# Attention: the products with picked probabilities are issued half a step later, right ahead of the next weighted products

## The chip, the cores and the metric

The kernel runs on one core of one Trainium2 chip. The metric is the device time of one execution in microseconds (us). The engines have short names in what follows: PE is TensorE, DVE is VectorE, ACT is ScalarE, POOL is GpSimd and SP is SyncE, which issues most of the transfers.

## The reference

Two graph layers are applied, one after the other, to 16 samples of 512 nodes with 128 features each. The first one (two rounds of masked softmax over a graph, a norm, a feed-forward part and a norm) is not touched by the change. The second one is attention with eight heads in which the entry of an integer matrix, `adj`, says which of four value projections an edge uses:

```python
scores = jnp.einsum('bhid,bhjd->bhij', q, k) / np.sqrt(dh)
attn = jax.nn.softmax(scores, axis=-1)
for r in range(Wv.shape[0]):
    v_r = (src @ Wv[r] + bv[r]).reshape(Bb, Nn, h, dh).transpose(0, 2, 1, 3)
    mask = (adj_matrix == r)[:, None]
    out = out + jnp.einsum('bhij,bhjd->bhid', attn * mask, v_r)
attn_out = out.transpose(0, 2, 1, 3).reshape(Bb, Nn, Dm) @ Wo + bo
x = _ln(src + attn_out, g1, beta1)
```

A last feed-forward part and a norm follow. In the data here `adj` holds 0 and 1 alone.

## The kernel before, in words

The kernel has three stages: `graph_layer`, `attention` and `feed_forward`. The change lies in `attention`, which takes about 640 us of the span.

`attention` has two paths and picks one at run time. Path 0 serves inputs with the codes 0 and 1 alone, and it is the one that runs here. It computes `prob` times `val` (the **weighted products**, value projection 0) plus `picked` times `dval` (the **products with picked probabilities**, with `picked = prob * mask` and the difference of projections 1 and 0).

A sample is worked on in a *turn* of eight *steps* (S = 8). Step s stands for head group g = s // 4 (four heads) and key chunk c = s % 4 (128 keys). For every step there are:

- four *peaks* (`peaks`, L990 to L1001 on PE): a bf16 product into `peak[hh % 2]`, of which DVE takes the maximum (L1248). They run six steps ahead of the scores, and there are two `peak` banks. So PE's peak number n waits until DVE has read peak n - 2.
- two *scores* (`scores`, L1015): two bf16 products each. ACT takes their exponential into `prob[s % 2]` (`exps`, L1113).
- `pick`: `picked[s % 2] = prob * mask`. POOL does three heads (L1384) in its step s, DVE the fourth (L1262) in its step s + 1.
- `weigh` (L1019 to L1042 on PE): eight f32 instructions on tiles 32 columns wide, all into `o_ps`, once with `prob` and `val` (`rel` is None) and once with `picked` and `dval` (`rel` is 0). The four chunks of a group accumulate in `o_ps`, and then ACT copies it out (`keep_o`, L1116 to L1124).
- *items*: the other work of the sample, one or two to a step, after a table. On PE every one of them writes the one bank `misc`, so each first waits on `misc_read`: until ACT or DVE has read the item before it. The place of an item in a step is "early", "mid" or "late":

```python
0: [(0, "mid", "q", 2), (1, "mid", "k", 2), (2, "early", "top1", 0), (2, "late", "v0", 1), (3, "mid", "o1", -1),
    (4, "early", "turn_o", -1), (4, "mid", "out", -1), (5, "mid", "y", -1), (6, "early", "top0", 1),
    (6, "late", "v1", 1), (7, "mid", "o0", 0)],
```

The order of each engine is written out by hand in a function `turn`. With P0 to P3 for the peaks, S0 and S1 for the scores, W for the weighted products and Wp for the picked ones, PE's step s (L1082 to L1098) is

P0, S0, [early item], P1, W of step s - 1, P2, S1, [mid item], P3, Wp of step s - 1, [late item].

DVE's step s is: read P0, read P1, pick of step s - 1, early item, read P2, read P3, mid item (L1343 to L1362). In step 5 it adds `norm_stats` (L1323, L1328). ACT's step s is: `exps` of S0, the late item of the step before, early item, in some steps part of a cast or of a mask, `exps` of S1, mid item, `keep_o`, and in steps 0 and 7 `centre` (L1196).

The readers of the items are: q and k, ACT L1134 and then DVE L1300; top0 and top1, DVE L1291 and L1293; v0 and v1, ACT L1142 and L1143; o0 and o1, DVE L1306 and L1310; turn_o, ACT L1155; out, DVE L1314; y, ACT L1157, after the second `exps` of its step.

The semaphore `picked_used` counts the Wp blocks that PE has done. Before the change it guards `picked` (for DVE and POOL) and also `prob`: `exps` of step s waits for Wp of step s - 2.

Of the kernel before, what the change touches and what calls it, by code (L numbers as in the profile page):

```python
# [821 lines left out]
def attention(nc, block, z, w, xs, codes, other, scratch, first_qk, sem, keep):  # L822
# [13 lines left out]
    with ExitStack() as ctx:  # L836
# [3 lines left out]
        def ps(name, shape, dt=F32):  # L840
            return ctx.enter_context(nc.psum_tensor("b_" + name, shape, dt))

        B, N, D, C, H, DH, R = z.B, z.N, z.D, z.C, HEADS, z.DH, z.R
# [44 lines left out]
            0: [(0, "mid", "q", 2), (1, "mid", "k", 2), (2, "early", "top1", 0), (2, "late", "v0", 1), (3, "mid", "o1", -1),  # L888
                (4, "early", "turn_o", -1), (4, "mid", "out", -1), (5, "mid", "y", -1), (6, "early", "top0", 1),
                (6, "late", "v1", 1), (7, "mid", "o0", 0)],  # L890
            1: [(0, "mid", "q", 2), (0, "late", "v0", 0), (0, "late", "v1", 0), (0, "late", "v2", 0), (0, "late", "v3", 0),
                (1, "mid", "k", 2), (2, "early", "top1", 0), (3, "mid", "o1", -1), (4, "early", "turn_o", -1),
                (4, "mid", "out", -1), (5, "mid", "y", -1), (6, "early", "top0", 1), (7, "mid", "o0", 0)],
        }
# [35 lines left out]
        def moved(b, par, s, by):  # L930

            return b + (s + by) // S, (par + (s + by) // S) % 2, (s + by) % S
# [50 lines left out]
        def _(pe):  # L983
# [3 lines left out]
            def run(path, rels):  # L987
                NR = len(rels)

                def peaks(b, par, s, hh):  # L990

                    b, par, s = moved(b, par, s, LEAD)
                    if not live(b):
                        return
                    g, c = s // C, s % C
                    h = GH * g + hh
                    if s == 0 and hh == 0:
                        pe.wait_ge(sem("stacked"), 32 * (b + 1))
                    past(pe, sem("peak_read"), (S * b + s) * GH + hh - 1)
                    pe.matmul(peak[hh % 2][:, :], q_stack[par][0:K, h, c * P:(c + 1) * P], k_stack[par][0:K, h, :],  # L1000
                              start=True, stop=True).then_inc(sem("peak_ready"), 1)  # L1001

                def scores(b, par, s, u):

                    if not live(b):
                        return
                    g, c = s // C, s % C
                    if isinstance(b, int) and b == 0 and s == 0 and u == 0:
                        pe.wait_ge(consts, 4 + R)
                    if c == 0 and u == 0:  # L1010
                        pe.wait_ge(sem(f"tops_in{g}"), 32 * (b + 1))
                    past(pe, sem("exp_ready"), 2 * (S * b + s) + u - 1)
                    for k in range(2):
                        h = GH * g + 2 * u + k
                        mm = pe.matmul(score[u][:, k, :], k_stack[par][:, h, c * P:(c + 1) * P], q_stack[par][:, h, :],  # L1015
                                       start=True, stop=True)
                    mm.then_inc(sem(f"score_ready{u}"), 1)

                def weigh(t, par, s, rel):  # L1019

                    b, par, s = moved(t, par, s, -1)
                    if not live(b):
                        return
                    g, c = s // C, s % C
                    if rel is None:
                        pe.wait_ge(sem("exp_ready"), 2 * (S * b + s) + 2)
                        if s == 0:

                            pe.wait_ge(sem("misc_read"), reads_before(path, *((b - 1, "v1") if path == 0 else (b, "v3"))) + 1)
                        if c == 0:  # L1030
                            past(pe, sem("o_t_ready"), G * b + g)
                        src, v = prob[s % 2], val[par]
                    else:
                        n = NR * (S * b + s) + rel
                        pe.wait_ge(sem("picked_pool"), POOL_HEADS * (n + 1))
                        pe.wait_ge(sem("picked_dve"), (GH - POOL_HEADS) * (n + 1))
                        src, v = picked[(NR * s + rel) % 2], dval[par if path == 0 else rel]
                    for hh in range(GH):
                        mm = pe.matmul(o_ps[32 * hh:32 * hh + 32, :], v[:, c, GH * g + hh, :], src[:, hh, :],  # L1039
                                       start=(c == 0 and rel is None), stop=(c == C - 1 and rel == NR - 1))  # L1040
                    if rel is not None:
                        mm.then_inc(sem("picked_used"), 1)  # L1042

                def item(t, name, by):
                    b = t + by
                    if not live(b):
                        return

                    past(pe, sem("misc_read"), reads_before(path, t, name))
                    if name in ("q", "k"):  # L1050
                        mm = pe.matmul(misc[:, :], w["w" + name][:, :], xs[:, b, :, :].rearrange("p c d -> p (c d)"),
                                       start=True, stop=True)
                    elif name[0] == "v":

                        pe.wait_ge(sem("x_own"), 16 * (b + 1))
                        per, rs = (2, 2) if path == 0 else (1, R)
                        for k in range(per):
                            c = per * int(name[1]) + k
                            at = misc[:, k * rs * D:(k + 1) * rs * D]
                            pe.matmul(at, w["ones"][:, :], w["bias3"][:, 0:rs * D], start=True, stop=False)  # L1060
                            mm = pe.matmul(at, x_own[:, c * P:(c + 1) * P], w["wv"][:, 0:rs, :].rearrange("p r d -> p (r d)"),
                                           start=False, stop=True)
                    elif name[:3] == "top":
                        g = int(name[3])
                        pe.wait_ge(sem("peak_read"), (S * b + (g + 1) * C) * GH)
                        mm = pe.transpose(misc[0:GH * C, 0:P], top[g][:, :, :].rearrange("p h c -> p (h c)"), ident[:, :])
                    elif name in ("o0", "o1"):
                        g = int(name[1])
                        pe.wait_ge(sem("o_t_ready"), G * b + g + 1)
                        for c in range(C):  # L1070
                            mm = pe.transpose(misc[:, c * P:(c + 1) * P], o_t[g][:, c * P:(c + 1) * P], ident[:, :])
                    elif name == "turn_o":
                        for c in range(C):
                            mm = pe.transpose(misc[:, c * P:(c + 1) * P], o[:, c, :], ident[:, :])
                    elif name == "out":
                        mm = pe.matmul(misc[:, :], w["wo"][:, :], o_all_t[:, :], start=True, stop=True)
                    elif name == "y":
                        for c in range(C):
                            mm = pe.transpose(misc[:, c * P:(c + 1) * P], y_t[:, c * P:(c + 1) * P], ident[:, :])
                    mm.then_inc(sem(name + "_done"), 1)  # L1080

                def turn(b, par):  # L1082
                    for s in range(S):
                        peaks(b, par, s, 0)
                        scores(b, par, s, 0)
                        for name, by in items(path, s, "early"):
                            item(b, name, by)
                        peaks(b, par, s, 1)
                        weigh(b, par, s, None)
                        peaks(b, par, s, 2)  # L1090
                        scores(b, par, s, 1)
                        for name, by in items(path, s, "mid"):
                            item(b, name, by)
                        peaks(b, par, s, 3)
                        for rel in range(NR):
                            weigh(b, par, s, rel)
                        for name, by in items(path, s, "late"):
                            item(b, name, by)  # L1098
                turns(pe, turn)
            both_paths(pe, run)  # L1100

        @block.scalar
        def _(act):
            def run(path, rels):
                NR = len(rels)

                def exps(b, s, u):
                    if not live(b):
                        return
                    if u == 0:  # L1110
                        past(act, sem("picked_used"), NR * (S * b + s - 1))
                    act.wait_ge(sem(f"score_ready{u}"), S * b + s + 1)
                    act.activation(prob[s % 2][:, 2 * u:2 * u + 2, :], score[u][:, :, :], ACT.Exp,  # L1113
                                   scale=float(DH) ** -0.5).then_inc(sem("exp_ready"), 1)

                def keep_o(b, par, s):  # L1116

                    b, par, s = moved(b, par, s, -1)
                    if not live(b) or s % C != C - 1:
                        return  # L1120
                    g = s // C
# [76 lines left out]

                def turn(b, par):
                    for s in range(S):  # L1200
                        exps(b, s, 0)
                        if path == 0 and s > 0:
                            for name, by in items(path, s - 1, "late"):
# [11 lines left out]
                            load_tops(b, par, name, by)  # L1215
                        for name, by in items(path, s, "mid"):
                            item(b, par, name, by)
                        keep_o(b, par, s)
                        if path == 1:
                            for name, by in items(path, s, "late"):  # L1220
                                item(b, par, name, by)
# [419 lines left out]
```

## Time and profile before

| | us |
|---|---|
| median of 3 runs | 1255.81 (1253.42 to 1255.83) |
| the profiled execution | 1248.62, of which 1246.8 span |
| busy over the span | PE 87%, DVE 77%, ACT 61%, POOL 49% |
| granted TensorE clock, mean over the span | 0.96 |

The page is read so: "busy" is the union of an engine's instructions. For PE the ends are modelled and instructions overlap, so the distance from one start to the next is the better price. In rows of the timeline the first number is the start in us, the second the length of the merged run, and the number in square brackets is the idle time ahead of it, with what ended it.

### The profile page before, as it was taken

How to read it: one execution, taken by the hardware profiler on the slowest of the kernel's cores; microseconds unless marked ns; L12 is line 12 of the kernel's file. 1: busy time of each engine (PE TensorE's matmuls, PEld its weight loads, DVE VectorE, ACT ScalarE, POOL GpSimd, SP SyncE). 2: the span in 40 equal slices, each digit the busy share in tenths (PEclk: the TensorE clock that was granted, in tenths of full speed). 3: DMA queues.
4: the chain of work that ended last, by engine and by line, in shares of the span. 5: the costliest groups of instructions: out<-in, count | busy, mean ns of one | idle time of the engine just before them, and what ended most of it. 6: DMA issues, size and time to landing. Idle time of an engine off the chain costs nothing. (4 is left out here: it accounts for less than half of the span.)

```text
span 1246.8 us, 21668 instructions
## 1 busy us (share of the span) xinstructions
PE 1087.4 (87%) x6087; PEld 500.5 (40%) x6087; DVE 956.3 (77%) x2313; ACT 758.9 (61%) x1405; POOL 610.5 (49%) x499
## 2 busy tenths in 40 slices
PE   4588877888787649999999999999999999979996
PEld 3565665665564312233333333323333233234442
DVE  2878778778877548788888888888888888618777
ACT  3477677777777324666666666666666666644442
POOL 3313212212300135878887788877888787900000
PEclk8699999999999858999999999999999999979998
DMA  5221112112100242321333213332133320000000
GB/s 171 89 86 68 50 66 86 50 50 101 50 1 1 85 117 72 106 76 43 109 110 105 66 49 110 110 98 68 54 110 110 90 71 9 2 0 34 34 34 34
DMA packets 49413, 86.50 MB, mean 69 GB/s; under 512 B 8787, under 2 KB 35795, under 8 KB 44246
## 3 DMA queue, kind: packets, MB, share of 16 engines
q1 hardware_dynamic: 46454, 85.56, 22.2%
q10 hardware_dynamic: 2912, 0.40, 0.2%
q8 instruction: 20, 0.33, 0.1%
q14 instruction: 27, 0.22, 0.1%
HBM read 52.12 MB, written 29.36 MB: 65 GB/s over the span
## 5 line engine op out<-in xcount | busy, mean ns | idle before, releaser
L1384 POOL TENSOR_TENSOR b_picked<-b_prob,b_mask 128x512 f32<-128x512 f32 x384 | 473.4, 1260 | 128.2 <-ACT b_prob L1113 128.1
L1248 DVE TENSOR_REDUCE b_top<-b_peak 128x1 f32<-128x512 f32 x512 | 343.1, 687 | 86.2 <-PE b_peak L1000 81.5
L1113 ACT ACTIVATE b_prob<-b_score 128x1024 f32<-128x1024 f32 x256 | 262.0, 1023 | 192.7 <-PE b_score L1015 190.8
L381 POOL TENSOR_SCALAR a_code<-a_adj_in 128x512 bf16<-128x512 int32 x64 | 89.0, 1391 | 249.2 <-DMA a_adj_in<-in_adj 245.4
L1039 PE MATMUL b_o_ps<-b_picked,b_dval 128*32 128x512 f32 x1024 | 136.4, 604 | 12.8 <-DVE b_picked L1262 10.2
L1039 PE MATMUL b_o_ps<-b_prob,b_val 128*32 128x512 f32 x1024 | 136.3, 604 | 0.3 <-ACT b_o_t L1124 0.3
L1262 DVE TENSOR_TENSOR b_picked<-b_prob,b_mask 128x512 f32<-128x512 f32 x128 | 113.5, 886 | 1.5 <-ACT b_prob L1113 1.4
L1000 PE MATMUL b_peak<-shared 96*128 96x512 bf16 x256 | 101.3, 399 | 4.7 <-DVE b_top L1248 4.5
L678 DVE CUSTOM_DVE_ANT_0 a_att<-a_att,a_no_edge 128x512 f32<-128x512 f32 x128 | 102.2, 816 | 0.0
L1000 PE MATMUL b_peak<-b_k_stack,b_q_stack 96*128 96x512 bf16 x256 | 98.3, 384 | 0.0
L650 ACT ACTIVATE a_att<-a_att,a_least 128x512 f32<-128x512 f32 x128 | 90.6, 711 | 0.0
L493 PE MATMUL a_turn<-a_hw_n,a_att 128*128 128x128 f32 x512 | 62.3, 281 | 25.7 <-ACT a_hw_n L599 25.6
L1501 ACT ACTIVATE c_hid<-c_mid,bff 128x512 f32<-128x512 f32 x64 | 44.0, 687 | 61.9 <-PE c_mid L1479 61.9
L1015 PE MATMUL b_score<-b_q_stack,b_k_stack 98*128 98x512 bf16 x256 | 76.5, 379 | 0.0
L1015 PE MATMUL b_score<-shared 98*128 98x512 bf16 x256 | 76.4, 379 | 0.0
L493 PEld LDWEIGHTS a_turn<-a_hw_n,a_att 128*128 128x128 f32 x512 | 59.7, 195 | 38.0 <-issue 38.0
L485 PE MATMUL a_out<-a_hid,wff 128*128 128x512 f32 x128 | 59.2, 605 | 18.0 <-ACT a_hid L644 18.0
L479 PE MATMUL a_mid<-a_h_t,wff 128*128 128x512 f32 x128 | 63.0, 617 | 11.1 <-ACT a_h_t L569 11.1
L1000 PEld LDWEIGHTS b_peak<-shared 96*128 96x128 bf16 x256 | 25.0, 98 | 113.0 <-DVE b_top L1248 98.6
L1000 PEld LDWEIGHTS b_peak<-b_k_stack,b_q_stack 96*128 96x128 bf16 x256 | 24.6, 96 | 108.8 <-DVE b_top L1248 93.8
L503 PE MATMUL a_pair<-a_xw_n,a_att 128*128 128x130 f32 x512 | 62.0, 280 | 3.4 <-DVE a_xw_n L710 3.4
L503 PEld LDWEIGHTS a_pair<-a_xw_n,a_att 128*128 128x128 f32 x512 | 60.5, 196 | 3.8 <-issue 3.8
(176 smaller groups left out, 1703.2 us busy)
## 6 DMA issues: line engine op xcount, KB each, us to landing
a_adj_in<-in_adj SPq DMA_DIRECT2D x16, 1024.0 KB, 5.2
scratch<-shared SPq DMA_DIRECT2D x32, 384.0 KB, 2.7
shared<-scratch SPq DMA_DIRECT2D x16, 768.0 KB, 6.7
scratch<-shared SPq DMA_DIRECT2D x32, 256.0 KB, 2.8
b_q_stack<-scratch SPq DMA_DIRECT2D x8, 768.0 KB, 5.4
b_k_stack<-scratch SPq DMA_DIRECT2D x8, 768.0 KB, 8.1
a_x_in<-in_x SPq DMA_DIRECT2D x16, 256.0 KB, 2.7
xs<-in_x SPq DMA_DIRECT2D x16, 256.0 KB, 5.3
```

Of the source, the lines that this page charges most:

```text
L381: eng.tensor_scalar(code[:, c, :].rearrange("p (k q) -> p k q", k=C), adj_in[:, c, :].rearrange("p (q k) -> p k q", k=C), CODE_HI, CODE_LO ...
L493: mm = pe.matmul(turn[:, ic * D:(ic + 1) * D], att[1][:, jc, ic * P:(ic + 1) * P], hw_n[:, jc, :], start=(jc == 0), stop=(jc == C - 1))
L503: mm = pe.matmul(pair[:, ic // 2, at:at + D + 2], att[0][:, jc, ic * P:(ic + 1) * P], xw_n[:, jc, :], start=(jc == 0), stop=(jc == C - 1))
L650: act.activation(att[k][:, c, :], att[k][:, c, :], ACT.Exp, bias=least[k][:, c:c + 1], scale=-1.0, accum_out=total[k][:, c:c + 1]).then_in ...
L678: dve.tensor_tensor_reduce(att[k][:, c, :], att[k][:, c, :], no_edge[:, c, :], 1.0, HIGHEST, ALU.add, ALU.min, least[k][:, c:c + 1]).then_ ...
L1000: pe.matmul(peak[hh % 2][:, :], q_stack[par][0:K, h, c * P:(c + 1) * P], k_stack[par][0:K, h, :], start=True, stop=True).then_inc(sem("pea ...
L1015: mm = pe.matmul(score[u][:, k, :], k_stack[par][:, h, c * P:(c + 1) * P], q_stack[par][:, h, :], start=True, stop=True)
L1039: mm = pe.matmul(o_ps[32 * hh:32 * hh + 32, :], v[:, c, GH * g + hh, :], src[:, hh, :], start=(c == 0 and rel is None), stop=(c == C - 1 a ...
L1113: act.activation(prob[s % 2][:, 2 * u:2 * u + 2, :], score[u][:, :, :], ACT.Exp, scale=float(DH) ** -0.5).then_inc(sem("exp_ready"), 1)
L1248: dve.tensor_reduce(top[g][:, hh, c:c + 1], peak[hh % 2][:, :], AX.X, ALU.max, negate=True).then_inc(sem("peak_read"), 1)
L1262: dve.tensor_tensor(picked[(NR * s + rel) % 2][:, hh, :], prob[s % 2][:, hh, :], m, ALU.mult).then_inc(sem("picked_dve"), 1)
L1384: pool.tensor_tensor(picked[(NR * s + rel) % 2][:, hh, :], prob[s % 2][:, hh, :], m, ALU.mult).then_inc(sem("picked_pool"), 1)
```

## The change

Wp in PE's step s is now that of step s - 2. It is issued right ahead of W, behind P1, except in steps 1 and 5 (`s % C == 1`), in which it is issued at the very start, ahead of P0. The order of PE is then:

- steps 1 and 5: Wp of s - 2, P0, S0, [early], P1, W of s - 1, P2, S1, [mid], P3, [late];
- the six others: P0, S0, [early], P1, Wp of s - 2, W of s - 1, P2, S1, [mid], P3, [late].

W now increments a semaphore of its own, `weighed`. `exps` waits for `weighed` and for POOL's and DVE's picks of step s - 2 in place of `picked_used`. `keep_o` moves from the end of ACT's step to the start of the next one. The rest of the diff puts the value items of path 1, which doesn't run here, into the next step.

```diff
-            1: [(0, "mid", "q", 2), (0, "late", "v0", 0), (0, "late", "v1", 0), (0, "late", "v2", 0), (0, "late", "v3", 0),
+            1: [(0, "mid", "q", 2), (1, "early", "v0", 0), (1, "early", "v1", 0), (1, "early", "v2", 0), (1, "early", "v3", 0),
...
                 def weigh(t, par, s, rel):
 
-                    b, par, s = moved(t, par, s, -1)
+                    b, par, s = moved(t, par, s, -1 if rel is None else -2)
...
-                    if rel is not None:
-                        mm.then_inc(sem("picked_used"), 1)
+                    mm.then_inc(sem("weighed" if rel is None else "picked_used"), 1)
...
                 def turn(b, par):
                     for s in range(S):
+                        ends = s % C == 1
+                        if ends:
+                            weigh_picked(b, par, s)
                         peaks(b, par, s, 0)
                         scores(b, par, s, 0)
                         for name, by in items(path, s, "early"):
                             item(b, name, by)
                         peaks(b, par, s, 1)
+                        if not ends:
+                            weigh_picked(b, par, s)
                         weigh(b, par, s, None)
                         peaks(b, par, s, 2)
                         scores(b, par, s, 1)
                         for name, by in items(path, s, "mid"):
                             item(b, name, by)
                         peaks(b, par, s, 3)
-                        for rel in range(NR):
-                            weigh(b, par, s, rel)
                         for name, by in items(path, s, "late"):
                             item(b, name, by)
+
+                def weigh_picked(b, par, s):
+
+                    for rel in range(NR):
+                        weigh(b, par, s, rel)
...
                     if u == 0:
-                        past(act, sem("picked_used"), NR * (S * b + s - 1))
+                        past(act, sem("picked_pool"), POOL_HEADS * NR * (S * b + s - 1))
+                        past(act, sem("picked_dve"), (GH - POOL_HEADS) * NR * (S * b + s - 1))
+                        past(act, sem("weighed"), S * b + s - 1)
...
                 def keep_o(b, par, s):
 
-                    b, par, s = moved(b, par, s, -1)
+                    b, par, s = moved(b, par, s, -2)
...
                 def turn(b, par):
                     for s in range(S):
+                        keep_o(b, par, s)
                         exps(b, s, 0)
...
                         for name, by in items(path, s, "mid"):
                             item(b, par, name, by)
-                        keep_o(b, par, s)
```

## Rows read from the trace of the kernel before

**Rows 1.** Steady attention: busy us (instructions) of PE, PEld, DVE, ACT, POOL; clock; DMA

```profile
485.30:1053.40 568.10, 558.33 (x3318) 174.04 (x3316) 481.50 (x866) 369.19 (x572) 463.40 (x380) 1.00 0.29 84
```

**Rows 2.** Waits in attention: us in total, times, longest

```profile
PE b_o_ps L1039 <- DVE b_picked L1262: 10.2, 15, 0.8
```

**Rows 3.** Timeline of PE, steps 5 and 6 of one turn

```profile
697.70 0.60 PE L1079 MATMUL b_misc<-ident,shared 128*128 128x128 f32 x4
698.13 0.38 PE L1000 MATMUL b_peak<-shared 96*128 96x512 bf16 x1
698.45 1.06 PE L1039 MATMUL b_o_ps<-b_picked,b_dval 128*32 128x512 f32 x8
699.44 0.39 PE L1000 MATMUL b_peak<-shared 96*128 96x512 bf16 x1
699.67 0.60 PE L1015 MATMUL b_score<-b_q_stack,b_k_stack 98*128 98x512 bf16 x2
700.11 0.27 PE L1066 MATMUL b_misc<-ident,b_top 128*16 128x128 f32 x1
700.22 0.38 PE L1000 MATMUL b_peak<-shared 96*128 96x512 bf16 x1
...
703.25 1.06 PE L1039 MATMUL b_o_ps<-b_picked,b_dval 128*32 128x512 f32 x8 [0.69 <-DVE b_picked L1262]
```

**Rows 4.** Timeline of PE, the two halves of one W block

```profile
706.31 0.64 PE L1039 MATMUL b_o_ps<-b_prob,b_val 128*32 128x512 f32 x4
...
706.76 0.61 PE L1039 MATMUL b_o_ps<-b_prob,b_val 128*32 128x512 f32 x4
```

**Rows 5.** Timeline, item k of step 1 and who reads it

```profile
717.17 1.02 PE L1051 MATMUL b_misc<-xs,wk 128*128 x2
...
718.03 0.38 PE L1000 MATMUL b_peak<-shared 96*128 96x512 bf16 x1
718.29 0.68 ACT L1134 ACTIVATE shared<-b_misc,bk 128x512 bf16<-128x512 f32 x1
...
718.45 0.69 DVE L1248 TENSOR_REDUCE b_top<-b_peak 128x1 f32<-128x512 f32 x1 [0.82 <-PE b_peak L1000]
719.06 0.75 DVE L1300 SCALAR_TENSOR_TENSOR shared<-b_misc,bk,shared 128x512 f32<-128x512 f32 x1
```

**Rows 6.** Timeline, P3 of step 3 and DVE's read of item o1

```profile
727.65 0.38 PE L1000 MATMUL b_peak<-b_k_stack,b_q_stack 96*128 96x512 bf16 x1
...
728.96 0.42 DVE L1310 TENSOR_TENSOR shared<-b_misc,b_inv 128x256 f32<-128x256 f32 x1
```

**Rows 7.** Timeline, ACT, DVE and POOL behind item y of step 5

```profile
698.82 0.58 ACT L1157 COPY b_y<-b_misc 128x512 f32<-128x512 f32 x1
...
701.40 3.83 POOL L1384 TENSOR_TENSOR b_picked<-b_prob,b_mask 128x512 f32<-128x512 f32 x3 [0.71 <-ACT b_prob L1113]
...
701.95 1.16 DVE L1262 TENSOR_TENSOR b_picked<-b_prob,b_mask 128x512 f32<-128x512 f32 x1
...
703.34 0.28 DVE L1293 TENSOR_TENSOR b_top_lo<-b_misc,b_top_hi 16x128 bf16<-16x128 f32 x1
```

**Rows 8.** All picks of DVE: duration ns min/median/max, first and last start

```profile
L1262 DVE TENSOR_TENSOR b_picked<-b_prob,b_mask x128: 681/683/1548, 484.3 to 1090.5; 128x512 f32<-128x512 f32 x128
```

**Rows 9.** Timeline ahead of the first step, when peaks wait for DVE's reads

```profile
466.26 0.68 DVE L1248 TENSOR_REDUCE b_top<-b_peak 128x1 f32<-128x512 f32 x1
...
467.00 0.61 PE L1000 MATMUL b_peak<-shared 96*128 96x512 bf16 x1 [0.21 <-DVE b_top L1248]
```

**Rows 10.** Timeline around the copy of o_ps in steps 0 and 1

```profile
713.52 0.69 ACT L1134 ACTIVATE shared<-b_misc,bq 128x512 bf16<-128x512 f32 x1
...
714.68 0.59 ACT L1124 COPY b_o_t<-b_o_ps 128x512 f32<-128x512 f32 x1 [0.47 <-PE b_o_ps L1039]
715.16 0.88 ACT L1196 ACTIVATE xs<-b_y,b_shift,b_rstd 128x128 f32 x2
...
715.51 1.07 PE L1039 MATMUL b_o_ps<-b_prob,b_val 128*32 128x512 f32 x8
```

## The prediction

> **What bounds the kernel now.** I read the busy time by stretches first. In the steady part of attention PE is busy 558.33 of 568.10 us at the full granted clock, DVE 481.50, POOL 463.40, ACT 369.19 [rows 1]. So PE sets the pace there, and all its idle time is 9.8 us. The view of waits says where that is: Wp waits for DVE's pick, 15 times, 10.2 us [rows 2]. The timeline shows it at one place of each turn, step 6 [rows 3]. The other waits fall on weight loads, which lie beside running products. PE therefore gets faster only if its stream gets shorter, and slower by every wait that is put into it. Prices on PE are start to start.
>
> **What the change takes away.** (a) The wait of Wp in step 6: Wp of step 4 stands there now, whose pick was made a step earlier. That is 10.2 us [rows 2], if nothing behind it waits for the same chain.
>
> (b) Changes between tile shapes. A peak before S0 costs 0.23 (699.44 to 699.67), and before Wp 0.32 (698.13 to 698.45) [rows 3]: 0.09 more to go to 32-column tiles. A block of eight costs 0.99 up to the peak (698.45 to 699.44) [rows 3], but its two halves are 0.45 apart [rows 4], so 2 x 0.45 = 0.90 would do: 0.09 more to leave. With Wp and W adjacent, one entry and one exit vanish: 0.18 per merged step. There are 127 Wp blocks with a W of the next step behind them; those in steps 1 and 5 aren't merged, which leaves 96: 96 x 0.18 = 17.3 us. No row shows two blocks in a row, so the price is bounded: 0 if the second block pays the same again, 17.3 if it costs its halves alone. I take 17.3, since all eight instructions have the shape of those before them, as the two halves do.
>
> The Trainium skill (TensorEngine Tiling (Array Packing), Key Properties) says that changing the tiling mode, and not just the tile, drains TensorE. The two 0.09 us agree. By that rule, which speaks of the switch and not of waits, the change is a gain; it is the first rival.
>
> **What the change puts in.** A Wp block stood between P3 of a step and P0 of the next, and gave DVE and ACT 1.0 us to read what the mid item and P3 had left. It is gone from there in six of eight transitions. From P3 to an early item is now P3, P0, S0, so 0.22 + 0.22 + 0.44 = 0.88 (S0's two instructions of 512 columns take 0.44, 699.67 to 700.11, a peak is one such [rows 3]); before it was 0.32 + 0.99 + 0.67 = 1.98. DVE's order isn't changed. Every item waits for the reader of the one before it, as there is one `misc` bank. From the end of a read, 466.26 + 0.68 = 466.94, to the peak that waited for it, at 467.00, it takes 0.06 [rows 9]; from the pick's end, 703.11 [rows 7], to Wp at 703.25 [rows 3] it takes 0.14. I take 0.06 for peaks and 0.1 for items.
>
> - Step 1 to 2, top1 behind k. k starts at 717.17, P3 0.86 later, ACT's part at 718.29, DVE's read of P3 at 718.45, DVE's read of k from 719.06 to 719.81 [rows 5]: 2.64 behind k. top1 could start 0.86 + 0.88 = 1.74 behind k, but is released at 2.74. Wait 1.00, 14 turns: 14.0.
> - Step 3 to 4, turn_o behind o1. P3 at 727.65, DVE's last read of o1 from 728.96 to 729.38 [rows 6], so 1.73 behind P3, 1.83 with the release, against 0.88. Wait 0.95, 15 turns: 14.3.
> - Step 5 to 6, top0 behind y. y starts at 697.70, P3 0.43 later [rows 3]; ACT copies y until 699.40 [rows 7], 1.70 behind y; released at 1.80 against 0.43 + 0.88 = 1.31. Wait 0.49, 14 turns: 6.9.
> - Step 6, v1 behind top0. DVE reads top0 behind its pick, and norm_stats of y stands ahead of its reads; that chain makes today's wait of Wp. It ends at 703.62 [rows 7], 5.92 behind y, so v1 is free at 6.02. In the new order top0 is at 1.80, P1 1.91, Wp 2.22, W 3.12, P2 4.11, S1 4.34, P3 4.78, v1 5.00. Wait 1.02. But the pick takes 1.16 there [rows 7] where 0.68 is the least [rows 8]; it starts 0.55 into POOL's first multiply and ends 0.55 behind that one's end (3.83 / 3 = some 1.2 each). POOL starts that multiply at 3.70 now; in the new order it must wait until Wp of step 4 has freed `picked`: 2.22 + 1.06 + 0.08 = 3.36. Then all ends 0.34 earlier. Wait 0.68, 14 turns: 9.5. So (a) is not gained: the wait moves from Wp to v1.
> - Step 7 to 0, P1. It needs DVE's read of P3, which starts 0.42 behind P3 and takes 0.69 [rows 5], with the release 1.17, against 0.88. Wait 0.29, 15 turns: 4.4. P0 needs only the read of P2, and its own natural distance from P2 is at least 1.3 (S1, the mid item, P3) against 1.17. Where a late item or Wp (steps 0 and 4) stands between, none waits.
> - Step 1, keep_o. It now stands behind `centre`: behind q's part (ends 714.21), 0.88 of `centre`, 0.59 of copy [rows 10] gives 715.68, released 715.78, and by the overlap of ACT's starts some 0.17 less; W is due at 715.51. I take 0.2, 14 turns: 2.8.
>
> Sum put in: 14.0 + 14.3 + 6.9 + 9.5 + 4.4 + 2.8 = 51.9. Sum taken out: 10.2 + 17.3 = 27.5. Net **24 us slower**: 1248.6 + 24.4 = 1273.0 for the profiled execution. The median of the runs stands 7.2 above that execution, so 1255.8 + 24.4 = **1280**.
>
> At nothing I cost: the looser guard of `prob` (exps start behind the scores anyway); the semaphore of W; POOL's later start in merged steps, which has 1 us spare per step (463.40 busy of 568.10 [rows 1]) and a step more until PE needs it; the stacks' and tops' transfers, which keep their places in their queues and whose takers come later, not earlier, in a longer turn. If POOL's cover were gone, Wp would wait for it at 1.2 us a multiply.
>
> **The rivals.**
> *Only the gain (faster).* The early items and v1 don't wait, because the reads end sooner than I say, once PE's blocks lie elsewhere. Place: top1, turn_o, top0, v1. Point: it decides if all four reads end within 0.88 of P3. Price: -27.5, so 1228. For it: in the trace of now Wp alone waits by any length [rows 2]. The Trainium skill's rule on mode changes (TensorEngine Tiling (Array Packing), Key Properties) speaks for it too. Against it: DVE starts each read only behind its read of P3, which alone ends 1.11 behind it [rows 5].
> *No saving at the merge (slower still).* The second block pays entry and exit again: 17.3 less gained, 1280 + 17 = 1297.
> *Waits half as long (about none).* If DVE and ACT drift ahead and the waits come to 26, the sum is -1.5: 1254. Against it: the chains hang on PE's own k, y and P3, so they can't drift.
>
> **How the numbers follow.** Forecast 0.72 (1280); only the gain 0.08; no saving 0.13; half as long 0.07. The range leaves out the first rival and the far end of the second: below, the waits at two thirds (-17) give 1263; above, two thirds of the missing saving give 1292 and the coarse release times a little more: 1262 to 1294. A measurement can tell about 0.2% (2.5 us) from no change. Slower has forecast, second rival and a third of the last, 0.87; same 0.04; faster 0.09.
>
> **What would show it.** Right: a turn is some 1.7 us longer than before; PE idles before L1066 (on DVE L1300, and ACT L1157), before L1074 (on DVE L1310), before L1060 in step 6 (on DVE L1293), and before P1 of step 0; Wp waits for nothing; Wp to W is 0.90. Wrong: Wp to W at 1.0 or more; early items starting 0.44 behind S0; a wait of Wp on POOL.

## The result, and the profile after the change

The changed kernel takes 1267.74 us (median of 4 runs, 1265.18 to 1270.88) against 1254.62 us for the kernel before (4 runs). The ratio is 1.0123, with a 95% interval of 1.0097 to 1.0149: **slower by 15 us, between 12 and 19**. The prediction was 1280, 24 us slower, with a range of 1262 to 1294. Direction and mechanism held; the size was too large by half.

The profiled execution took 1267.58 us, with a span of 1265.7. Its span is 18.9 us above that of before, more than the runs show; the profiled execution of before was 7 us below its own median, and 3.2 of the 18.9 lie ahead of the first Wp. The steadier measure within a profile is the stretch from the first to the last Wp. These are the rows of L1039, first of the kernel before, then of the changed one (duration min/median/max in ns, then the first and the last start):

```profile
L1039 PE MATMUL b_o_ps<-b_picked,b_dval x1024: 589/593/617, 485.9 to 1094.2; 128*32 128x512 f32 x171
```

```profile
L1039 PE MATMUL b_o_ps<-b_picked,b_dval x1024: 589/593/618, 489.1 to 1112.8; 128*32 128x512 f32 x171
```

608.3 us have become 623.7, 15.4 more, which is what the runs say. I call this the *Wp stretch* below.

The busy time in a window of the steady part, to be held against [rows 1]. The window is longer (584.70 us), as it ends about where the same work now ends. PE is busy for 546.30 of it, no longer for 98% but for 93%. DVE has the same 481 us of work as before:

```profile
485.30:1070.00 584.70, 546.30 (x3314) 187.86 (x3314) 481.21 (x864) 370.20 (x570) 456.25 (x379) 1.00 0.29 82
```

The waits of PE in attention (total us, times, longest). The 10.2 us of [rows 2] are gone. In their place stand five others, all but one on an item that waits for the reader of the item before. The fifth is on a peak:

```profile
PE b_misc L1065 <- DVE shared L1309: 11.8, 14, 0.9
PE b_misc L1073 <- DVE shared L1319: 11.0, 15, 0.8
PE b_misc L1059 <- DVE b_top_lo L1302: 9.7, 14, 0.7
PE b_misc L1065 <- ACT b_y L1166: 4.0, 14, 0.3
PE b_peak L1000 <- DVE b_top L1257: 4.0, 12, 1.4
```

(L1065 is the transpose of top1 or top0, L1073 turn_o, L1059 v0 or v1. The idle time counted here begins at the modelled end of the product ahead, so it is less than the distance from start to start. That distance is used from here on.)

The timeline of PE through step 6, against [rows 3], with its idle times in square brackets:

```profile
705.03 0.60 PE L1078 MATMUL b_misc<-ident,shared 128*128 128x128 f32 x4
705.47 0.60 PE L1000 MATMUL b_peak<-shared 96*128 96x512 bf16 x2
705.90 0.60 PE L1015 MATMUL b_score<-b_q_stack,b_k_stack 98*128 98x512 bf16 x2
706.78 0.28 PE L1065 MATMUL b_misc<-ident,b_top 128*16 128x128 f32 x1 [0.28 <-ACT b_y L1166]
706.90 0.38 PE L1000 MATMUL b_peak<-shared 96*128 96x512 bf16 x1
707.21 1.06 PE L1039 MATMUL b_o_ps<-b_picked,b_dval 128*32 128x512 f32 x8
708.09 1.04 PE L1039 MATMUL b_o_ps<-b_prob,b_val 128*32 128x512 f32 x8
709.06 0.39 PE L1000 MATMUL b_peak<-shared 96*128 96x512 bf16 x1
...
709.73 0.38 PE L1000 MATMUL b_peak<-shared 96*128 96x512 bf16 x1
710.81 0.28 PE L1059 MATMUL b_misc<-bias,ones 128*128 128x256 bf16 x1 [0.71 <-DVE b_top_lo L1302]
```

What to see: P3 and P0 are one run of two (705.47), with no block between them. top0 starts 0.88 behind S0, where 0.44 would do. Wp does not wait, and W follows it after 0.88. Then v1 stands 1.08 behind P3 for a distance of 0.22: the wait of Wp has become a wait of v1, 0.87 long.

The reader's side of the largest wait, item k and top1, against [rows 5]:

```profile
725.49 0.38 PE L1000 MATMUL b_peak<-shared 96*128 96x512 bf16 x1
...
725.75 0.68 ACT L1143 ACTIVATE shared<-b_misc,bk 128x512 bf16<-128x512 f32 x1
...
725.90 0.69 DVE L1257 TENSOR_REDUCE b_top<-b_peak 128x1 f32<-128x512 f32 x1 [0.82 <-PE b_peak L1000]
...
726.52 0.75 DVE L1309 SCALAR_TENSOR_TENSOR shared<-b_misc,bk,shared 128x512 f32<-128x512 f32 x1
...
727.41 0.27 PE L1065 MATMUL b_misc<-ident,b_top 128*16 128x128 f32 x1 [0.89 <-DVE shared L1309]
```

DVE's read of k starts 1.03 behind P3 and ends at 1.78, as it did before the change (719.06 and 719.81 behind 718.03). PE would arrive 1.1 us earlier than in the old order, and waits until 0.14 beyond the end of the read. The lengths of this wait that the prediction took over from the trace of before have stayed.

### The profile page after: what moved, and what is told of

It reads as the page before. It is cut to its first block and busy times, and to the rows that moved or that the text cites. A ratio compares the mean times of both kernels' runs of the same rounds, so it can differ in the third digit from the quotient of the medians.

```text
span 1265.7 us, 21884 instructions
## 1 busy us (share of the span) xinstructions
PE 1076.9 (85%) x6087; PEld 515.2 (41%) x6087; DVE 957.2 (76%) x2313; ACT 760.0 (60%) x1405; POOL 605.4 (48%) x499
## 5 line engine op out<-in xcount | busy, mean ns | idle before, releaser
L1393 POOL TENSOR_TENSOR b_picked<-b_prob,b_mask 128x512 f32<-128x512 f32 x384 | 466.6, 1238 | 153.8 <-ACT b_prob L1122 77.6
L1039 PE MATMUL b_o_ps<-b_picked,b_dval 128*32 128x512 f32 x1024 | 136.4, 604 | 3.0 <-POOL b_picked L1393 1.7
L1039 PE MATMUL b_o_ps<-b_prob,b_val 128*32 128x512 f32 x1024 | 134.1, 595 | 0.3 <-ACT b_o_t L1133 0.3
L1000 PE MATMUL b_peak<-b_k_stack,b_q_stack 96*128 96x512 bf16 x256 | 94.5, 383 | 1.9 <-DVE b_top L1257 0.5
```

The source lines that it names most:

```text
L1393: pool.tensor_tensor(picked[(NR * s + rel) % 2][:, hh, :], prob[s % 2][:, hh, :], m, ALU.mult).then_inc(sem("picked_pool"), 1)
```

## The experiments

Each kernel's own waits are read from its timeline, as the distance from start to start less that of the same pair where nothing waits. "Behind before" is its ratio to the kernel before.

### The old order alone put back (e1_order_back)

```diff
-                        ends = s % C == 1
-                        if ends:
-                            weigh_picked(b, par, s)
...
-                        if not ends:
+                        if s in ():
                             weigh_picked(b, par, s)
...
                         peaks(b, par, s, 3)
+                        if (s + 1) % S not in ():
+                            weigh_picked(b + (s + 1) // S, (par + (s + 1) // S) % 2, (s + 1) % S)
```

(`s in ()` is never true, so no Wp stands ahead of W.)

> The changed kernel with TensorE's old order alone put back (Wp of step s-1 behind P3); the new guards of prob, the semaphore of W and the new place of keep_o stay. Theory (all of the loss is PE's order: six gaps between a mid item and the next early item or peak lost the block that filled them): the time of the kernel before, within 3 us, 14 to 15 waits of Wp for DVE's pick of 0.76 again, no wait ahead of top1, turn_o, top0. Rival (the guards or keep_o behind centre cost something): stays 3 to 12 us above the kernel before.

Ratio 0.9987 (0.9967 to 1.0008): no different from the kernel before. Its Wp stretch is 608.1 us, and the only wait over 0.1 us that recurs in each turn is that of Wp in step 6, 14 times, 0.76. So the whole loss is PE's order; the new guards of `prob`, the semaphore and the new place of `keep_o` cost nothing that the runs can tell. That settles the theory against its rival.

### One merge alone (e4_merge2)

Against e1_order_back:

```diff
-                        if s in ():
+                        if s in (2,):
                             weigh_picked(b, par, s)
                         weigh(b, par, s, None)
...
                         peaks(b, par, s, 3)
-                        if (s + 1) % S not in ():
+                        if (s + 1) % S not in (2,):
                             weigh_picked(b + (s + 1) // S, (par + (s + 1) // S) % 2, (s + 1) % S)
```

> As e1_order_back, but Wp of step 0 alone is moved, ahead of W in step 2, in every turn. Theory: PE waits some 1.05 us ahead of top1 in step 2, 15 times, and gains 0.2 us by the merge, 16 times; the other waits of the changed kernel do not appear: 12 to 13 us slower than the kernel before. Rival one (the loss is spread over all merges alike): a sixth of the loss, 2 us slower. Rival two (a merge only saves): 3 us faster.

Ratio 1.0105 (1.0077 to 1.0132), 13 us slower (10 to 17). Its Wp stretch is 617.8 us, 9.5 longer than before, against 15.4 for all six merges. So one merge of six brings most of the loss, as what the others cost is for the larger part covered by what they save. PE in steps 1 and 2:

```profile
724.05 1.02 PE L1050 MATMUL b_misc<-xs,wk 128*128 x2
724.91 0.38 PE L1000 MATMUL b_peak<-shared 96*128 96x512 bf16 x1
725.13 0.38 PE L1000 MATMUL b_peak<-b_k_stack,b_q_stack 96*128 96x512 bf16 x1
725.34 0.59 PE L1015 MATMUL b_score<-shared 98*128 98x512 bf16 x2
726.83 0.27 PE L1065 MATMUL b_misc<-ident,b_top 128*16 128x128 f32 x1 [0.89 <-DVE shared L1308]
726.94 0.38 PE L1000 MATMUL b_peak<-b_k_stack,b_q_stack 96*128 96x512 bf16 x1
727.25 1.06 PE L1039 MATMUL b_o_ps<-b_picked,b_dval 128*32 128x512 f32 x8
728.13 1.04 PE L1039 MATMUL b_o_ps<-b_prob,b_val 128*32 128x512 f32 x8
```

top1 starts 1.49 behind S0 instead of 0.44, 1.05 late, and the merge gives back 0.24. The waits of Wp in step 6 are still there, and none of turn_o or top0. Both rivals fall.

### DVE reads o1 earlier (e3_o1_ahead)

```diff
                         peaks(b, par, s, 2)
+                        if s == 3:
+                            for name, by in items(path, s, "mid"):
+                                item(b, name, by)
                         peaks(b, par, s, 3)
-                        for name, by in items(path, s, "mid"):
-                            item(b, name, by)
+                        if s != 3:
+                            for name, by in items(path, s, "mid"):
+                                item(b, name, by)
```

> The changed kernel with one edit on VectorE: in step 3 it reads item o1 (reciprocal and product) ahead of its read of P3, not behind it. Theory (turn_o waits for that read alone): the wait ahead of turn_o falls from 0.92 to about 0.2 us, P1 of step 4 waits up to 0.2 more for the read of P3 that is now later, so some 0.5 us less in 15 turns: 7 us faster than the changed kernel. Rival (VectorE as a whole is late there, whatever its order): the wait moves to P1 of step 4 in full, no gain.

The wait ahead of turn_o fell from 0.92 to 0.10, and P1 behind it starts 0.16 late where it had been 0.05: 0.71 us less in a steady turn. The Wp stretch is 613.9 us, 9.8 less than the changed kernel's 623.7. The runs give a ratio of 1.0085 (1.0056 to 1.0114), 5 us better than the changed kernel's 1.0123, with intervals that overlap, so that the gain rests on the traces. turn_o waits for DVE's order, not for a lack of DVE's time.

### DVE picks ahead of the norm (e2_pick_ahead)

```diff
-                        if path == 0:
+                        if path == 0 and s != 6:
                             pick(b, par, s)
...
                         if s == 5:
+                            if path == 0:
+                                pick(b, par, 6)
                             norm_stats(b)
```

> The changed kernel with one edit on VectorE: its pick for step 5 stands ahead of norm_stats, at the end of its step 5, not in its step 6. Theory (v1 waits for the chain y, ACT's copy, norm_stats, two reads, pick, top0's reads): that chain loses the pick's 0.7 to 1.2 us, of which some 0.4 to 0.6 come back as norm_stats starts later; the wait ahead of v1 falls from 0.87 to about 0.3 us: 7 us faster than the changed kernel. Rival (v1 waits because Wp is gone from in front of it, whatever VectorE does first): no gain.

The wait ahead of v1 fell from 0.87 to 0.21, as expected. But P2 of step 6 now waits 0.34 for DVE's read of P0, which had not been expected: the pick pushes norm_stats, and norm_stats pushes the reads. The Wp stretch is 619.3 us, 4.4 better; the ratio is 1.0104 (1.0074 to 1.0134), not told apart from 1.0123 by the runs. v1's wait is the chain's, but half of what is taken off it comes back two peaks earlier.

### The same edit on the kernel before (n1_pick_ahead)

> The kernel before with the one edit of e2_pick_ahead: VectorE's pick for step 5 stands ahead of norm_stats. TensorE's order is the old one. Theory (the only wait of TensorE in the steady part is Wp of step 6 for the chain y, copy, norm_stats, two reads, pick): the 14 waits of 0.76 us vanish and none takes their place, as the old order leaves 1.0 us between P3 and P0: 10 us faster than the kernel before, ratio 0.992. Rival (the chain is only turned round: norm_stats starts later and P2 of step 6 or v1 waits in its place): less than 4 us faster.

Ratio 0.9977 (0.9961 to 0.9992), 3 us faster: the rival was right. The timeline shows the new wait, now in front of P2 in step 6, 0.56 from start to start. (The pick took 0.96 here, beside a multiply of POOL.)

```profile
697.75 0.96 DVE L1262 TENSOR_TENSOR b_picked<-b_prob,b_mask 128x512 f32<-128x512 f32 x1
...
698.62 0.86 DVE L1323 BATCH_NORM_STATS2 b_stats<-b_y 128x6 f32<-128x128 f32 x4
...
699.93 1.28 DVE L1248 TENSOR_REDUCE b_top<-b_peak 128x1 f32<-128x512 f32 x2
...
700.68 0.39 PE L1000 MATMUL b_peak<-shared 96*128 96x512 bf16 x1 [0.50 <-DVE b_top L1248]
```

### The merge made the other way round (n3_w_late)

```diff
                         peaks(b, par, s, 1)
-                        weigh(b, par, s, None)
                         peaks(b, par, s, 2)
...
                         peaks(b, par, s, 3)
+                        weigh(b, par, s, None)
                         for rel in range(NR):
                             weigh(b, par, s, rel)
```

> The kernel before with the merge made the other way round: W of step s-1 is issued behind P3, right ahead of Wp of the same step, in all eight steps; nothing stands between P1 and P2. Theory (a merge gains 0.2 us; what counts is who loses the cover): 127 merges gain 26 us and the distance from a mid item to the next early one grows, so no wait ahead of top1, turn_o, top0 from the step before; but P2 must wait for the read of P0 (0.3 us in the steps without an early item, 5 of 8: 24 us) and out for ACT's copy of turn_o (some 0.7 us, 15 times: 10 us). Sum about 8 us slower than the kernel before, waits ahead of P2 and L1076 instead. Rival (a merge that keeps the cover behind P3 has no price): 26 us faster.

Ratio 1.0290 (1.0249 to 1.0332), 36 us slower; over four times what was expected. The waits named were there (P2 0.29, out 0.45), but I had missed the largest: o0 and o1 wait 0.8 us each for ACT's copies of v0 and v1, which had been covered by W between P1 and P2, and P2 of step 6 waits 0.89 for reads behind norm_stats.

```profile
PE b_misc L1071 <- ACT b_dval L1143: 17.2, 26, 1.0
```

So the gap from a late item to the next mid item needs its block as much as that from a mid item to the next early one. The old order had one block in each.

### Early items moved behind W (e5_items_behind_w)

The changed kernel, with this on PE:

```diff
-                        for name, by in items(path, s, "early"):
-                            item(b, name, by)
                         peaks(b, par, s, 1)
                         if not ends:
                             weigh_picked(b, par, s)
                         weigh(b, par, s, None)
+                        for name, by in items(path, s, "early"):
+                            item(b, name, by)
                         peaks(b, par, s, 2)
```

> The changed kernel with TensorE's early items (top1, turn_o, top0) moved behind W of their step, so that 2.1 us more lie between a mid item and the early item. Theory (each early item waits for the reader of the item before; P1 next in line waits for the read of P3): the waits ahead of top1 (1.05), turn_o (0.92) and top0 (0.44) vanish, P1 waits 0.29 in steps 2, 4 and 6, out waits 0.3 for ACT's copy, v1 waits 1.2 in place of 0.87 as its chain has not moved: 0.7 us less a turn, 10 us faster than the changed kernel. Rival (VectorE has too much work between P3 and P2, so the whole wait reappears ahead of P1 and P2): no gain.

Ratio 0.9996 (0.9978 to 1.0015): 15 us faster than the changed kernel in the traces (608.6 us of Wp stretch), and level with the one before. top1, turn_o and top0 wait no more. What is left is what was expected, P1 0.30 in the three steps and out 0.26, with a small wait of v0, 0.12, that was not. But v1 waits 0.76 and not 1.2, which is most of why 15 us came and not 10. The merge itself is all there. This shows that the loss was the place of the items against the blocks, and not DVE's amount of work.

### Taking norm_stats off the chain (n4_norm_late, e6_both, n5_norm_split, e7_both_split)

On the kernel before and on e5_items_behind_w, norm_stats goes to DVE's step 6, and rstds, shifts and centre one step on. n4 and e6 do all four chunks of centre in step 0; n5 and e7 do two there and two in step 3:

```diff
-                        if s == 5:
+                        if s == 6:
                             norm_stats(b)
-                        if s == 6:
+                        if s == 7:
                             shifts(b - 1)
...
-                        if s == 6:
+                        if s == 7:
                             rstds(b - 1)
...
                         if s == 0:
+                            centre(b - 2, (0, 1))
+                        if s == 3:
                             centre(b - 2, (2, 3))
-                        if s == 7:
-                            centre(b - 1, range(C) if isinstance(b, int) and b == B else (0, 1))
+                        if s == 7 and isinstance(b, int) and b == B:
+                            centre(b - 1, range(C))
```

> The kernel before, TensorE's order untouched, with norm_stats moved from VectorE's step 5 to its step 6, behind the mid items, and rstds, shifts and centre moved one step on with it (all four chunks of centre in step 0). Theory (the wait of Wp in step 6 is norm_stats, 1.3 us, in front of the reads of P0 and P1): the 14 waits of 0.76 us vanish; in step 7 VectorE has no pick behind it that TensorE needs within 1.3 us, so none takes their place: 10 us faster than the kernel before, ratio 0.992. Rival (VectorE is short of time anywhere, since n1_pick_ahead gave back 0.56 of 0.76): a wait of P0 or P1 in step 7 of 0.3 us or more, less than 6 us faster.

> e5_items_behind_w and the move of norm_stats of n4_norm_late together. Theory: the chain of v1 loses norm_stats, so its wait falls from 1.2 to under 0.4: 11 us faster than e5_items_behind_w, close to the kernel before (within 5 us), and still behind n4_norm_late by some 8 us, since the waits of P1 (0.29, 4 places) and out cost more than six merges of 0.21 bring. Rival (with the items out of the way the merge pays): faster than n4_norm_late.

n4: ratio 1.0012 (0.9997 to 1.0027). The wait of Wp was gone, but top1 waited 0.68 in its place. ACT's centre now took 1.65 us (the rows below, of n4's timeline) where it had taken 0.88 [rows 10], so exps of step 1 and k's part, and with them DVE's read of k, came late. e6: 1.0103 (1.0074 to 1.0132), the waits by the same centre being v0 0.92 and W of step 1 0.74; P0 of step 0 waits 0.52 besides, for a read of DVE. Both expectations missed ACT.

```profile
720.83 1.65 ACT L1196 ACTIVATE xs<-b_y,b_shift,b_rstd 128x128 f32 x4
722.38 1.00 ACT L1113 ACTIVATE b_prob<-b_score 128x1024 f32<-128x1024 f32 x1
```

> n4_norm_late with centre divided again: chunks 0 and 1 in ScalarE's step 0, chunks 2 and 3 in its step 3. TensorE's order is the old one. In n4_norm_late the wait of Wp was gone, but top1 waited 0.68, as ScalarE's four chunks in step 0 made exps of step 1, and with it k's part, late. Theory: with two chunks there, as in the kernel before, top1 does not wait, and no wait over 0.1 is left in the steady part: 10 us faster than the kernel before, ratio 0.992. Rival (VectorE's norm_stats in step 6 costs by itself): 0 to 4 us faster.

> e6_both with the same division of centre, so the changed kernel with early items behind W and norm_stats in VectorE's step 6. In e6_both v1's wait was gone, but v0 waited 0.92, W of step 1 0.74 and P0 of step 0 0.52. Theory (the first two are ScalarE's four chunks of centre in step 0, the third is norm_stats ahead of the reads of step 7): v0's falls to 0.15 and W's to 0 to 0.3, P0's stays 0.52: 15 us faster than e6_both, and 3 us faster than the kernel before, still 7 us behind n5_norm_split. Rival (merging pays once the items are out of the way): as fast as n5_norm_split or faster.

**n5: ratio 0.9928 (0.9900 to 0.9956), 9 us faster than the kernel before**, and so 24 us faster than the changed one. As expected, no wait over 0.1 us is left that recurs in each turn. Its PE, in the window of [rows 1], is busy 566.82 of 568.10 us:

```profile
485.30:1053.40 568.10, 566.82 (x3358) 177.46 (x3357) 489.28 (x876) 372.60 (x575) 470.82 (x385) 1.00 0.30 85
```

e7: 0.9959 (0.9934 to 0.9984), 5 us faster than the kernel before. v0 waits 0.12, W of step 1 no more, and P0 of step 0 still 0.52, all as expected. Its Wp stretch is 602.6 us against 599.5 in n5, so with the items out of the way and the norm off the chain, the merged order is still a little behind the old one in the traces. The two intervals of the runs overlap.

## Why the prediction was right, and where its sizes were off

In the trace of the changed kernel the waits of PE in the Wp stretch add up to 52.9 us (15 of top1, 15 of turn_o, 14 or 15 each of top0, v1 and P1); the kernel before has 11.9.

| step of the prediction | predicted | measured |
|---|---|---|
| top1 behind k | 1.00 us, 14.0 in all | 1.05, 14.7 |
| turn_o behind o1 | 0.95, 14.3 | 0.92, 13.4 |
| top0 behind y | 0.49, 6.9 | 0.44, 6.2 |
| v1 behind top0 | 0.68, 9.5 | 0.87, 12.0 |
| P1 of step 0 | 0.29, 4.4 | 0.30, 4.5 |
| W behind keep_o in step 1 | 0.2, 2.8 | none |
| wait of Wp in step 6, removed | 10.2 | 10.9 |
| a merge | 0.18, 17.3 | 0.24, 23.0 |

**Right.** The five waits came at the places that were named, for the readers that were named, and within 0.05 us but for v1. They follow from two facts that need no measurement of the new order: which instruction frees the bank, and how far behind P3 it ends. e4_merge2, e3_o1_ahead and e5_items_behind_w show that it is this and not something that goes with it. The first step, (a), was right as well in its reserve: the wait of Wp was not gained but moved to v1. POOL, which was costed at nothing, waits for Wp now, 73 times. PE waits for POOL but once, 1.7 us at the end, where it had waited 2.4 before. ACT's `exps`, by their new guard, wait for it 7 times, 2.0 us in all:

```profile
POOL b_picked L1393 <- PE b_o_ps L1039: 75.6, 73, 1.8
```

**The terms that were mis-sized.** A merge saves 0.24 us, not 0.18, so 23.0 instead of 17.3, which the prediction had taken for the upper bound. The entry (0.31 before Wp against 0.22 before a peak) and the blocks were as said, but between two blocks in a row the tail is shorter than two halves (0.88 for 0.90), and the block behind leaves after 0.97 instead of 0.99 to 1.00. The term for keep_o was 2.8 too high. The prediction's own working (0.27 less 0.17) gave 0.1 and not the 0.2 that it took, and in the changed kernel `centre` had started at once behind q's part and the copy was done at 722.90, 0.07 ahead of W:

```profile
721.56 0.87 ACT L1205 ACTIVATE xs<-b_y,b_shift,b_rstd 128x128 f32 x2
...
722.33 0.57 ACT L1133 COPY b_o_t<-b_o_ps 128x512 f32<-128x512 f32 x1
...
722.97 0.64 PE L1039 MATMUL b_o_ps<-b_prob,b_val 128*32 128x512 f32 x4
```

v1's wait was 0.19 too low. POOL's first multiply of step 6 starts 3.51 behind y (708.54 less 705.03) and not 3.36, as it starts 0.27 behind the modelled end of Wp and not 0.08. So DVE's pick ends at 710.25, 5.22 behind y: 0.19 earlier than before, where I had reckoned 0.34. And PE came to P3 4.70 behind y, 0.08 earlier than reckoned.

```profile
708.54 2.72 POOL L1393 TENSOR_TENSOR b_picked<-b_prob,b_mask 128x512 f32<-128x512 f32 x2 [0.52 <-PE b_o_ps L1039]
```

```profile
709.28 0.97 DVE L1271 TENSOR_TENSOR b_picked<-b_prob,b_mask 128x512 f32<-128x512 f32 x1
```

That the sum of the waits put in came out so near (51.9, and 50.8 in the table) is in part luck: keep_o's 2.8 too much and v1's 2.5 too little cancel. What made the forecast too large is mainly the merge, by 5.7.

With the measured terms the sum is 52.9 - 11.9 - 23.0 = 18.0 us, against 15.4 in the Wp stretch and 12 to 19 in the runs. In a steady turn it closes better. From one top1 to the next it is 40.45 us (727.41 to 767.86), against 39.13 in the kernel before: 1.32 longer, where the prediction had said 1.7. The terms give 3.58 for the five waits, less 0.76 for Wp and 1.44 for six merges, so 1.38. Most of the 2.6 therefore lies in the first and last turns, where peaks or other parts are absent, and which this account doesn't split.

**The rivals.** "Only the gain" needed the reads to end within 0.88 us of P3. Those of k, o1 and y end 1.3 to 1.8 behind it, and that of top0 ends 1.03 behind a P3 that v1 could follow after 0.22. The rival's saving was real, though, and even larger than stated: e5_items_behind_w, in which the early items have got their distance back, is level with the kernel before, with v1 still waiting. e7_both_split is no further sign of it, as what puts it ahead of the kernel before is the norm's new place; against n5_norm_split, which has that too, its Wp stretch is 3.1 us longer. The Trainium skill's rule (TensorEngine Tiling (Array Packing), Key Properties: changing the tiling mode drains TensorE) is borne out in its direction by the 0.24 us. It says nothing of what the removed block had covered. "No saving at the merge" fell by the same rows. "Waits half as long" fell too: the least of the five, top0's, is 0.9 of its size.

## What to carry to other kernels

A block of products on a saturated TensorE is also a delay line. Before two blocks are joined, write down for each gap that loses one the chain that must end inside it (matmul, reader's start, reader's end, release), and compare it with what is left of the gap; the price of the gap that fails could be read from the old trace to 0.05 us in four of five cases here; the fifth, whose chain ran through POOL's start, was 0.19 off. When one wait is left, don't reorder the work in front of it but move the work that doesn't belong to its chain (here norm_stats), and check each engine that has to take it: ACT's step 0 had room for two chunks, not for four.

## What the runs showed of the hardware that was not expected

Two blocks of 32-column products in a row cost less than their halves apart would say. The halves of both blocks in the changed kernel start at 707.21, 707.66, 708.09 and 708.52:

```profile
707.66 0.61 PE L1039 MATMUL b_o_ps<-b_picked,b_dval 128*32 128x512 f32 x4
708.09 0.61 PE L1039 MATMUL b_o_ps<-b_prob,b_val 128*32 128x512 f32 x4
```

Only the first half after the change of shape takes 0.45; the later ones follow at 0.43. So some 0.02 of the price of a change lies in the first half behind it, and the last half takes 0.54 to the next peak. Why it does isn't settled by these runs.
